# First attention of a hybrid kernel: the roots of the router's norms moved from GpSimd to VectorE, and GpSimd's row transfers unpaced

## The chip, the cores and the metric

One core of a Trainium2 chip runs the whole program. The time is the device time of one execution in microseconds (us), as the median of several runs. A profile comes from one execution of its own. Engines are called by their names or by the profile's: PE (TensorE), DVE (VectorE), ACT (ScalarE), POOL (GpSimd), SP (SyncE, which only issues transfers here).

## The reference, cut to what matters

```python
x = L0_attn_a_x                                        # [16, 256, 128]
x = x + attn_a(layernorm(x), mask, w_q, w_k, w_v, w_o)  # 16 sequences, one head of 128
x = x + ffn(layernorm(x), ...)                          # mixture of 8 experts, top 2, and a shared one
x = x + attn_b(layernorm(x), ...)                       # 16 causal heads of 8
x = x + ffn(layernorm(x), ...)

def layernorm(x):                                       # eps = 1e-5
    return (x - mean(x)) / sqrt(var(x) + eps)

def ffn(x, ...):
    logits = x @ router_w                               # [4096, 8]
    # first and second expert of each row, its place in that expert's list (capacity 1280)
    combine, dispatch = top2_gating(logits, capacity)
    y = combine-weighted silu(x_e @ w1 + b1) @ w2 + b2  # per expert, over the rows sent to it
    return y + 0.1 * (silu(x @ sw1 + sb1) @ sw2 + sb2)
```

## The kernel before, in words

All 4096 rows of x stay in SBUF, as 32 tiles of 128 rows. The 16 sequences of the first attention are taken in 8 pairs; one pair is 4 tiles. The order of work on every engine is written out by hand: each engine has its own `attn_a_pair(i)` (PE from line 856, ACT from 1248, DVE from 1721), called for i = -2 to 7, and each runs its instructions strictly in that order, with semaphores between the engines.

In step i the engines work on several pairs at once. Sequence n = 2i and n + 1 get their probabilities transposed and multiplied with the values, n + 1 and n + 2 get their scores, n + 2 and n + 3 are projected. Behind the attention runs the router of the mixture, also pair by pair:

- In step i DVE takes the statistics of pair i after its attention was added (`stats2`, and `stats2_end`, line 1510, which writes `mv2`, mean and variance of 4 tiles).
- GpSimd makes the inverse roots `rstd2` from them (`rstd2_of`, line 587: an add of epsilon and a power of -0.5, on 128 x 4 numbers).
- In step i + 1 DVE normalizes the four tiles into `xr` (`norm_r`, line 1519, four instructions of which the first waits for the root), PE transposes them (`r_transpose`, line 816, the matmuls on line 825), ACT copies them, PE makes the logits (`r_logits`, line 832), DVE finds the first expert (`lead`, five small operations) and then the second (`second`, line 1557, eight small operations), each of which waits on a semaphore for the one before.
- In step i + 2 PE counts the places of the rows (`counts`) and DVE makes the slot numbers (`placed`, line 1588, five small operations). In that step they are interleaved with the four `norm_r` of the next pair: placed, norm, placed, norm and so on.
- GpSimd then sends the rows: `dispatch(0, k)`, line 596, k = 0 to 63. Each is one indirect transfer of 128 rows of `xr` to their slots in `x_slots` in HBM, eight per pair (four tiles, first and second expert). In `attn_a` (line 630) GpSimd starts with the roots of the first norms and of the first two router norms; then a loop over i = 2 to 7 places five to seven transfers per pair behind waits for the probabilities' transposes, projections and values of that pair, and the root of the next pair behind them. The transfers left over follow at the end.

The last pair's router work lies in the first items of the mixture (`moe`, DVE from line 1848).

The mixture of a layer runs over 56 items of 256 rows: 16 pieces through the shared expert and 40 chunks, five per expert, through the experts. The first ten items are pieces (0 to 9), then come the 40 chunks, then the last six pieces. PE does `first_mm(w)` (line 919, in 12 matmuls) and then `second_mm(w - 1)` (line 940, in 16). DVE splits the input of item w + 1 in a high and a low part (`x_split`, line 1704) and adds the output of item w - 1 (`y_copy`, line 1831). In step w = 9, ahead of the first chunk, DVE's order is the other way round: `y_copy` of item 8 (line 1856), and then `x_split` of chunk 0, which for a chunk also transposes it (line 1714).

The chunks are read back from `x_slots` by SP (`chunk_loads`) and, for half of the first chunk, ACT (`first_chunk`), once all 64 row transfers have landed.

In the second attention the router's roots stay with GpSimd (`rstd2_of`, `shift2_of`) in both kernels.

Of the kernel before, what the change touches and what calls it, by code (L numbers as in the profile page):

```python
# [51 lines left out]
LEAD, SECOND, PLACED = 5, 8, 5  # L52
LIMITS, GATES = 7, 14
# [37 lines left out]
def build(nc, x_in, hd_mask, w_q, w_k, w_v, w_o, attn_W, attn_b, out_W, out_b, router_w,  # L91
          w1, b1, w2, b2, sw1, sb1, sw2, sb2, out):
    with ExitStack() as ctx:
# [76 lines left out]

        x_cols = sb("x_cols", [P, 2, CH * P])
# [82 lines left out]
        S.xg_used = sem("xg_used")  # L254
        S.row_set = sem("row_set")
# [237 lines left out]
        def _(pool):  # L493
# [85 lines left out]
            def shift2_of(i):  # L579
# [4 lines left out]
                pool.wait_ge(S.ln2_rstd, PAIRS + i + 1)  # L584
                pool.tensor_tensor(nb2[:, :], nm2[:, :], rstd2[:, :], ALU.mult).then_inc(S.ln2_nb, 1)

            def rstd2_of(n):
                pool.wait_ge(S.ln2_mv, n)
                if n > PAIRS + 1:

                    pool.wait_ge(S.xn2_ready, n - 1)
                pool.tensor_scalar(ve2[:, :], mv2[:, :, 1], EPS, 1.0, ALU.add, ALU.mult).then_inc(S.ln2_ve, 1)
                pool.wait_ge(S.ln2_ve, n)
# [36 lines left out]
            def attn_a():  # L630
# [8 lines left out]
                for q in range(2, 7):  # L639
                    rstd_of(q, q + 1)  # L640
                rstd2_of(1)
                rstd_of(7, 8)
                rstd2_of(2)
                k = 0

                def row():
                    nonlocal k
                    dispatch(0, k)
                    k += 1


                for i in range(2, PAIRS):
                    n = 2 * i
                    if i > 2:
                        pool.wait_ge(S.probs_tr, n + 1)
                        row()
                        pool.wait_ge(S.gv_done, min(n + 3, SEQS))
                        row()
                    pool.wait_ge(S.y_done, n + 1)
                    row()  # L660
                    pool.wait_ge(S.probs_tr, n + 2)
                    row()
                    pool.wait_ge(S.gv_done, min(n + 4, SEQS))
                    row()
                    pool.wait_ge(S.y_done, n + 2)
                    row()
                    if i > 2:
                        row()
                    rstd2_of(i + 1)

                for k in range(k, 2 * NT):
                    dispatch(0, k)
# [807 lines left out]
        def _(dve):  # L1480
# [37 lines left out]

            def norm_r(n, j):
                t = 4 * (n % PAIRS) + j  # L1520
                if j == 0:
# [5 lines left out]
                    dve.wait_ge(S.ln2_rstd, n + 1)  # L1527
# [193 lines left out]
            def attn_a_pair(i):  # L1721
                n = 2 * i
                routed, led = valid(i - 2), valid(i - 1)
                if valid(i):
                    inverse_sums(n)
                if 0 <= n + 1 < SEQS:
                    maxes(n + 1)
                if valid(i):
                    add_attn(n)
                for j in range(PLACED):  # L1730
                    if routed:
                        placed(i - 2, j, bank[2])
                    if led and j < 4:
                        norm_r(i - 1, j)
# [399 lines left out]
```

## Time and profile before

| | |
|---|---|
| median of 3 runs | 770.65 us (766.17 to 772.09) |
| the profiled execution | 770.89 us |
| its span in the profile | 769.1 us |
| PE busy | 704.7 us (92%), 6152 matmuls |
| DVE busy | 523.9 us (68%), 1665 instructions |
| ACT busy | 449.7 us (58%) |
| POOL busy | 440.9 us (57%), 564 instructions |

The span runs from the first to the last instruction of the profiled execution; the device time adds 1.8 us around it. Busy time is the time in which an engine executes, its waits are left out. Shares are means over stages with different limits, so the rows below are taken from the stages that the change touches: the first attention (till about 103 us), the pieces (till about 138 us) and the start of the chunks (143 us).

### The profile page before, as it was taken

To read this page: it belongs to the slowest core of one execution; us is meant where nothing else is said; L and a number is where in the kernel's file an instruction comes from. 1 tells how busy PE (TensorE), PEld (TensorE's weight loads), DVE (VectorE), ACT (ScalarE), POOL (GpSimd) and SP (SyncE) were. 2 spreads that over 40 slices of the span, in tenths; PEclk is the share of its full clock that TensorE was granted. 3 is DMA by queue.
4 is the path that set the end of the run, shared out by engine and by line. 5 is a ranking of instruction groups with operands and counts; after the bars stand their busy time and mean duration, and the time that the engine had idled before them with its cause. 6 is when DMAs were issued, how large, how long until landed. Compare 5 with 4: busy or idle time off the path is not lost.

```text
span 769.1 us, 18168 instructions
## 1 busy us (share of the span) xinstructions
PE 704.7 (92%) x6152; PEld 641.6 (83%) x6152; DVE 523.9 (68%) x1665; ACT 449.7 (58%) x1144; POOL 440.9 (57%) x564
## 2 busy tenths in 40 slices
PE   6888789799999997889999998999999899999996
PEld 5777689799999996667777776777779899999996
DVE  5877765366556565768888988877676556655536
ACT  2565454344444443677878878787755444456545
POOL 6367777166666651344545767777777265666640
PEclk9999869999999998899999999999999999999999
DMA  7997111455556334333533434333201346555328
GB/s 245 309 323 183 46 48 55 58 113 108 108 99 133 78 104 118 104 99 109 142 101 91 126 119 147 100 95 111 62 30 53 53 84 131 109 97 112 90 68 287
DMA packets 167715, 89.35 MB, mean 116 GB/s; under 512 B 120576, under 2 KB 151890, under 8 KB 167528
## 3 DMA queue, kind: packets, MB, share of 16 engines
q1 hardware_dynamic: 155704, 69.89, 36.6%
q0 software_dynamic: 9216, 17.34, 6.6%
q10 hardware_dynamic: 2704, 0.98, 0.6%
q8 instruction: 50, 0.82, 0.5%
q14 instruction: 41, 0.34, 0.1%
HBM read 49.63 MB, written 39.67 MB: 116 GB/s over the span
## 4 chain that ended last, share of the span: by engine, by line
PE 57%; DVE 5%; POOL 5%; DMA 5%; SPq 4%; issue 4%; ACT 3%; ACTq 0%; DVEq 0%; POOLq 0%
PE bank L940 22%; PE bank L919 19%; PE bank L1021 4%; DMA qc<-qk_rows 3%; SPq L439 3%; POOL x_slots L611 3%; PE bank L980 2%; PE bank L998 2%; PE bank L1002 2%; POOL pt L695 2%; DVE negp L1951 1%; PE bank L976 1%; PE bank L981 1%; ACT pt L1389 1%; PE bank L1040 1%
## 5 line engine op out<-in xcount | busy, mean ns | idle before, releaser
L1291 ACT ACTIVATE hT<-bank,bias_T 128x256 f32<-128x256 f32 x448 | 175.7, 476 | 186.4 <-PE bank L919 186.3
L626 POOL DMA_INDIRECT y_rows<-yo,row_cur x160 | 158.5, 990 | 127.9 <-DVE yo L1845 103.2
L1951 DVE TENSOR_REDUCE negp<-bank 128x2 f32<-128x512 f32 (+1 forms) x192 | 129.6, 685 | 44.3 <-PE bank L981 27.1
L940 PE MATMUL bank<-w_s,hT 128*128 128x128 f32 x1280 | 155.9, 275 | 0.0
L611 POOL DMA_INDIRECT x_slots<-xr,slot_u x128 | 129.9, 1015 | 38.7 <-issue 35.5
L940 PEld LDWEIGHTS bank<-w_s,hT 128*128 128x128 f32 x1280 | 150.0, 192 | 0.0
L919 PE MATMUL bank<-xT_hl,w_hl 128*128 128x256 f32 x960 | 135.4, 291 | 9.1 <-DVE xT_hl L1719 9.1
L695 POOL TENSOR_SCALAR_AFFINE_SELECT pt<-pt 128x512 f32<-128x512 f32 x128 | 86.0, 680 | 92.7 <-ACT pt L1389 92.2
L1389 ACT ACTIVATE pt<-bank 128x512 f32<-128x512 f32 x192 | 107.8, 596 | 40.3 <-PE bank L1002 38.5
L919 PEld LDWEIGHTS bank<-xT_hl,w_hl 128*128 128x128 f32 x960 | 120.9, 192 | 9.6 <-issue 9.6
L1845 DVE TENSOR_TENSOR yo<-bank,b_b 128x256 f32<-128x256 f32 x80 | 33.9, 424 | 98.7 <-PE bank L940 98.7
L940 PE MATMUL bank<-sw_s,hT 128*128 128x128 f32 x512 | 63.0, 276 | 2.1 <-issue 2.1
L940 PEld LDWEIGHTS bank<-sw_s,hT 128*128 128x128 f32 x512 | 60.2, 193 | 2.8 <-issue 2.8
L1021 PE MATMUL bank<-pt,v_ext 128*32 128x256 f32 (+1 forms) x1024 | 55.5, 335 | 6.6 <-POOL pt L695 6.4
L919 PE MATMUL bank<-xT_hl,sw_hl 128*128 128x256 f32 x384 | 55.5, 296 | 2.1 <-issue 1.5
L919 PEld LDWEIGHTS bank<-xT_hl,sw_hl 128*128 128x128 f32 x384 | 49.8, 198 | 2.9 <-issue 2.1
L1021 PEld LDWEIGHTS bank<-pt,v_ext 128*32 128x32 f32 x1024 | 26.9, 110 | 27.8 <-POOL pt L695 10.4
L980 PE MATMUL bank<-bdk,qc 96*128 96x256 f32 x128 | 48.9, 382 | 1.1 <-DVE negp L1951 0.4
L998 PE MATMUL bank<-qc,bdk 128*128 128x256 f32 x256 | 41.5, 284 | 0.2 <-ACT pt L1389 0.2
L980 PEld LDWEIGHTS bank<-bdk,qc 96*128 96x128 f32 x128 | 25.6, 200 | 17.2 <-issue 8.7
L976 PE MATMUL bank<-bdk,qc 128*128 128x512 f32 x64 | 31.6, 493 | 8.9 <-DMA qc<-qk_rows 8.6
L1002 PE MATMUL bank<-qc,bdk 128*128 128x128 f32 x256 | 37.0, 267 | 2.9 <-ACT pt L1389 2.9
(214 smaller groups left out, 1194.0 us busy)
## 6 DMA issues: line engine op xcount, KB each, us to landing
xg_all<-x_slots SPq DMA_DIRECT2D x316, 32.0 KB
w_s<-in_L_ffn_w SPq DMA_DIRECT2D x32, 256.0 KB
qk_rows<-qks SPq DMA_DIRECT2D x16, 512.0 KB, 3.6
bdk<-qk_rows SPq DMA_DIRECT2D x187, 32.0 KB
qc<-qk_rows SPq DMA_DIRECT2D x45, 128.0 KB, 2.8
x_slots<-xg_all SPq DMA_DIRECT2D x1, 5440.0 KB, 21.7
y_rows<-xg_all SPq DMA_DIRECT2D x1, 4096.0 KB, 14.3
yab<-y_rows SPq DMA_DIRECT2D x16, 256.0 KB, 3.3
```

Source lines behind the costliest of these rows:

```text
L611: pool.indirect_dma_start(x_slots, bass.IndirectOffsetOnAxis(ap=slot_u[:, c, t:t + 1], axis=0), xr[:, t, :], None, bounds_check=last_slot, ...
L626: pool.indirect_dma_start(y_rows, bass.IndirectOffsetOnAxis(ap=row_cur[:, g % ROWS, j:j + 1], axis=0), yo[:, g % RING, j, :], None, bounds ...
L695: a = pool.affine_select(out=blk, in_=blk, compare_op=ALU.is_ge, fill=0.0, base=0, pattern=[[0, 4], [1, P]], channel_multiplier=-1)
L919: m = pe.matmul(bk[:, (f % 2) * 256:(f % 2) * 256 + 256], wt[:, wp, f * P:(f + 1) * P], xT_hl[:, w % 2, xp, :], start=(p == 0), stop=(p == 2))
L940: m = pe.matmul(yb(w, l)[:, j * P:(j + 1) * P], hT[:, w % 2, f, j * P:(j + 1) * P], wt[:, f, :], start=(f == 0), stop=(f == FT - 1))
L980: pe.matmul(halves[:, :, 0:P], q[0:96], heads[0:96, :, 0:P], start=True, stop=True)
L998: m = pe.matmul(bk[:, j * SEQ:j * SEQ + SEQ], bdk[:, par, g, 2 * k + j, 0:P], qc[:, par, g, :], start=True, stop=True)
L1002: m = pe.matmul(bk[:, j * P:j * P + P], bdk[:, par, g, j, P:SEQ], qc[:, par, g, P:SEQ], start=True, stop=True)
L1021: m = pe.matmul(OB[32 * j:32 * j + 32, c0 + kt * P:c0 + SEQ], v_ext[:, par, kt, 4 * g + j, :], rhs, start=(kt == 0 and g % 2 == 0), stop=( ...
L1291: a = act.activation(hT[:, w % 2, f, :], HB[2 * (w % 2) + f // 2][:, (f % 2) * 256:(f % 2) * 256 + 256], ACT.Silu, bias=bias_T[:, b0 + f:b ...
L1389: act.activation(pt[:, g % 2, k, :], CB[(g + k) % 2][:, :], ACT.Exp).then_inc(S.exp_done, 1)
L1951: dve.tensor_reduce(dst, AB[(g + k) % 2][:, :].rearrange("p (j k) -> p j k", j=heads), AX.X, ALU.max, negate=True).then_inc(S.amax_done, 1)
```

## The change

GpSimd's `attn_a` keeps the eight roots of the first norms and then issues the 64 transfers one after another, with no wait but those inside `dispatch` (for the pair's slot numbers). The eight roots of the router's norms of the first layer are made by DVE: `root_of(n, k)`, k = 0 to 8. Step 0 adds epsilon; step 1 makes a seed from the bits of the number, read as an integer (times -0.5 plus a constant, written as an integer); steps 2 to 5 are one refinement of higher order and steps 6 to 8 a second one. Each works on 128 x 4 numbers and each but the first waits for the one before through the semaphore `root`. They are interleaved with the other work of the pair: 0 and 1 at the end of step i, 2 to 8 in step i + 1. The four norms, which stood between the placing steps, come behind them. Beside this, the counts that GpSimd waits for in the second layer are shifted by eight.

```diff
--- before.py
+++ after.py
@@ -50,6 +50,8 @@
 WB_LOADS = 11
 QUAD = 4 * P
 LEAD, SECOND, PLACED = 5, 8, 5
+ROOT = 9
+ROOT_BITS = float(0x5F3759DF)
 LIMITS, GATES = 7, 14
 START = 4
 BY_SP = 7
@@ -168,6 +170,7 @@
         oT = sb("oT", [P, GRP, SEQ])
         on = sb("on", [P, 2, HEADS, HD]); onT = sb("onT", [P, SEQ]); osum = sb("osum", [P, 2, HEADS])
 
+        root_y = sb("root_y", [P, 2, 4]); root_t = sb("root_t", [P, 2, 4])
         x_cols = sb("x_cols", [P, 2, CH * P])
         xT_hl = sb("xT_hl", [P, 2, 2, CH * P], F32R)
         sw1_hl = sb("sw1_hl", [P, 2, F], F32R)
@@ -252,6 +255,7 @@
         S.slots2_even = sem("slots2_even")
         S.slots2_odd = sem("slots2_odd")
         S.xg_used = sem("xg_used")
+        S.root = sem("root")
         S.row_set = sem("row_set")
         S.xT_hi = sem("xT_hi")
         S.xT_ready = sem("xT_ready")
@@ -581,16 +585,14 @@
                 need(pool, S.xn2_ready, PAIRS + i)
                 pool.tensor_scalar(nm2[:, :], mv2[:, :, 0], -1.0, 1.0, ALU.mult, ALU.mult).then_inc(S.ln2_nm, 1)
                 pool.wait_ge(S.ln2_nm, i + 1)
-                pool.wait_ge(S.ln2_rstd, PAIRS + i + 1)
+                pool.wait_ge(S.ln2_rstd, i + 1)
                 pool.tensor_tensor(nb2[:, :], nm2[:, :], rstd2[:, :], ALU.mult).then_inc(S.ln2_nb, 1)
 
             def rstd2_of(n):
                 pool.wait_ge(S.ln2_mv, n)
-                if n > PAIRS + 1:
-
-                    pool.wait_ge(S.xn2_ready, n - 1)
+                pool.wait_ge(S.xn2_ready, n - 1)
                 pool.tensor_scalar(ve2[:, :], mv2[:, :, 1], EPS, 1.0, ALU.add, ALU.mult).then_inc(S.ln2_ve, 1)
-                pool.wait_ge(S.ln2_ve, n)
+                pool.wait_ge(S.ln2_ve, n - PAIRS)
                 pool.tensor_tensor(rstd2[:, :], ve2[:, :], neg_half[:, :], ALU.pow).then_inc(S.ln2_rstd, 1)
 
             def dispatch(l, k):
@@ -636,39 +638,9 @@
                 pool.wait_ge(S.ln_rstd, 2)
                 key_ones()
                 query_masks()
-                for q in range(2, 7):
+                for q in range(2, 8):
                     rstd_of(q, q + 1)
-                rstd2_of(1)
-                rstd_of(7, 8)
-                rstd2_of(2)
-                k = 0
-
-                def row():
-                    nonlocal k
-                    dispatch(0, k)
-                    k += 1
-
-
-                for i in range(2, PAIRS):
-                    n = 2 * i
-                    if i > 2:
-                        pool.wait_ge(S.probs_tr, n + 1)
-                        row()
-                        pool.wait_ge(S.gv_done, min(n + 3, SEQS))
-                        row()
-                    pool.wait_ge(S.y_done, n + 1)
-                    row()
-                    pool.wait_ge(S.probs_tr, n + 2)
-                    row()
-                    pool.wait_ge(S.gv_done, min(n + 4, SEQS))
-                    row()
-                    pool.wait_ge(S.y_done, n + 2)
-                    row()
-                    if i > 2:
-                        row()
-                    rstd2_of(i + 1)
-
-                for k in range(k, 2 * NT):
+                for k in range(2 * NT):
                     dispatch(0, k)
 
             def attn_b_consts():
@@ -1516,6 +1488,32 @@
                     a = dve.bn_aggr(mv2[:, j, :], st2[:, j, :])
                 a.then_inc(S.ln2_mv, 1)
 
+            def root_of(n, k):
+
+                y, t = root_y[:, 0, :], root_t[:, 0, :]
+                if k == 0:
+                    dve.wait_ge(S.ln2_mv, n + 1)
+                    a = dve.tensor_scalar(ve2[:, :], mv2[:, :, 1], EPS, None, ALU.add)
+                else:
+                    dve.wait_ge(S.root, ROOT * n + k)
+                if k == 1:
+                    a = dve.tensor_scalar(y.bitcast(I32), ve2[:, :].bitcast(I32), -0.5, ROOT_BITS, ALU.mult, ALU.add)
+                elif k == 2:
+                    a = dve.tensor_tensor(t, ve2[:, :], y, ALU.mult)
+                elif k == 3:
+                    a = dve.tensor_tensor(root_t[:, 1, :], t, y, ALU.mult)
+                elif k == 4:
+                    a = dve.scalar_tensor_tensor(out=t, in0=root_t[:, 1, :], scalar=-10.0 / 3.0, in1=root_t[:, 1, :], op0=ALU.add, op1=ALU.mult)
+                elif k == 5:
+                    a = dve.scalar_tensor_tensor(out=root_y[:, 1, :], in0=t, scalar=5.0, in1=y, op0=ALU.add, op1=ALU.mult)
+                elif k == 6:
+                    a = dve.tensor_tensor(t, ve2[:, :], root_y[:, 1, :], ALU.mult)
+                elif k == 7:
+                    a = dve.scalar_tensor_tensor(out=root_t[:, 1, :], in0=t, scalar=-0.5 * 0.375 ** 3, in1=root_y[:, 1, :], op0=ALU.mult, op1=ALU.mult)
+                elif k == 8:
+                    a = dve.scalar_tensor_tensor(out=rstd2[:, :], in0=root_t[:, 1, :], scalar=0.5625, in1=root_y[:, 1, :], op0=ALU.add, op1=ALU.mult)
+                a.then_inc(S.root, 1)
+
             def norm_r(n, j):
                 t = 4 * (n % PAIRS) + j
                 if j == 0:
@@ -1524,7 +1522,10 @@
                         dve.wait_ge(S.slots1, 512)
                         dve.wait_ge(S.slots2_even, 256)
                         dve.wait_ge(S.slots2_odd, 256)
-                    dve.wait_ge(S.ln2_rstd, n + 1)
+                    if n < PAIRS:
+                        dve.wait_ge(S.root, ROOT * (n + 1))
+                    else:
+                        dve.wait_ge(S.ln2_rstd, n - PAIRS + 1)
                 a = dve.tensor_scalar(xr[:, t, 0:D], x[:, t, :], mv2[:, j, 0:1], rstd2[:, j:j + 1], ALU.subtract, ALU.mult)
                 if j == 3:
                     a.then_inc(S.xn2_ready, 1)
@@ -1723,14 +1724,23 @@
                 routed, led = valid(i - 2), valid(i - 1)
                 if valid(i):
                     inverse_sums(n)
+                if led:
+                    root_of(i - 1, 2)
                 if 0 <= n + 1 < SEQS:
                     maxes(n + 1)
+                if led:
+                    root_of(i - 1, 3)
                 if valid(i):
                     add_attn(n)
+                if led:
+                    root_of(i - 1, 4)
                 for j in range(PLACED):
                     if routed:
                         placed(i - 2, j, bank[2])
                     if led and j < 4:
+                        root_of(i - 1, 5 + j)
+                if led:
+                    for j in range(4):
                         norm_r(i - 1, j)
                 if i == 0:
                     stats(4, 5)
@@ -1787,7 +1797,12 @@
                     stats2_end(i)
                 if led:
                     second(i - 1, 6)
+                if valid(i):
+                    root_of(i, 0)
+                if led:
                     second(i - 1, 7)
+                if valid(i):
+                    root_of(i, 1)
 
             for i in range(-2, PAIRS):
                 if i == -1:
@@ -1850,6 +1865,8 @@
                 for w in range(start, upto):
                     c = w - FRONT[l]
                     if l == 0 and w == 0:
+                        for k in range(2, ROOT):
+                            root_of(last, k)
                         for j in range(4):
                             norm_r(last, j)
                     if c == -1:
```

## Rows read from the trace of the kernel before

**Rows 1.** Busy time by engine (us, with instructions), PEclk granted clock; a middle and the last pair, chunk start
```profile
59.58:69.73 10.15, 8.70 (x69) 8.04 (x69) 8.15 (x44) 6.04 (x18) 8.02 (x9) 1.00 0.91 218
...
90.95:103.00 12.05, 8.78 (x42) 7.69 (x43) 8.00 (x42) 3.82 (x9) 8.28 (x9) 0.52 0.14 46
...
143.00:148.00 5.00, 5.00 (x32) 5.00 (x33) 1.42 (x5) 1.57 (x4) 0.00 (x0) 0.70 0.44 56
```

**Rows 2.** The chain that ended last: start us, us, what; 135 to 151
```profile
135.47 2.57 DMA x_slots<-xr,slot_u
...
141.50 0.46 DVE x_cols L1714
...
142.99 2.90 PE bank L919 x12
145.90 1.89 PE bank L940 x16
147.78 1.43 PE bank L919 x12
149.21 1.79 PE bank L940 x16
```

**Rows 3.** Timeline of PE around the first chunk: start us, us, line, operation, idle before
```profile
135.84 1.95 PE L940 MATMUL bank<-sw_s,hT 128*128 128x128 f32 x16
142.99 2.26 PE L919 MATMUL bank<-xT_hl,w_hl 128*128 128x256 f32 x9 [5.21 <-DVE xT_hl L1719]
```

**Rows 4.** GpSimd's transfers and roots, VectorE's norms by tile (ns min/median/max); one transfer
```profile
L611 POOL DMA_INDIRECT x_slots<-xr,slot_u x64: 967/974/1212, 42.9 to 135.5; - x64
...
L1528 DVE TENSOR_SCALAR xr<-x,mv,rstd x32: 331/340/528, 30.9 to 104.8; 128x128 f32<-128x128 f32 x32
...
L594 POOL TENSOR_TENSOR rstd<-ve,neg_half x8: 1009/1039/1040, 29.0 to 103.0; 128x4 f32<-128x4 f32 x8
...
64.90 0.97 POOL L611 DMA_INDIRECT x_slots<-xr,slot_u  x1 [0.30 <-issue]
```

**Rows 5.** Timeline of VectorE, the last pair's routing and before the first chunk
```profile
104.08 1.30 DVE L1528 TENSOR_SCALAR xr<-x,mv,rstd 128x128 f32<-128x128 f32 x4 [1.10 <-POOL rstd L594]
...
106.68 0.28 DVE L1599 TENSOR_REDUCE RR<-sel 128x16 f32<-128x128 f32 x1
107.00 0.17 DVE L1602 TENSOR_SCALAR far<-RR 128x8 f32<-128x8 f32 x1
107.21 0.16 DVE L1604 SCALAR_TENSOR_TENSOR slot_u<-RR,far 128x4 uint32<-128x4 f32 x1
...
117.38 0.18 DVE L1607 TENSOR_TENSOR slot_u<-RR,far 128x4 uint32<-128x4 f32 x1
...
137.83 0.42 DVE L1838 SCALAR_TENSOR_TENSOR x<-bank,x 128x256 f32<-128x256 f32 x1 [2.19 <-PE bank L940]
```

**Rows 6.** Timeline of VectorE, a middle pair of the first attention
```profile
59.50 0.16 DVE L1687 RECIPROCAL rsum<-psums 128x2 f32<-128x2 f32 x1
59.58 0.67 DVE L1682 TENSOR_REDUCE negmax<-bank 128x2 f32<-128x512 f32 x1
...
60.69 0.27 DVE L1595 TENSOR_TENSOR sel<-MK,bank 128x128 f32<-128x128 bf16 x1
...
62.12 0.34 DVE L1528 TENSOR_SCALAR xr<-x,mv,rstd 128x128 f32<-128x128 f32 x1
...
62.92 0.69 DVE L1682 TENSOR_REDUCE negmax<-bank 128x2 f32<-128x512 f32 x1 [0.30 <-PE bank L793]
```

**Rows 7.** Timeline of PE, the router's transposes of pair 1 and of a middle pair
```profile
32.22 0.60 PE L825 MATMUL bank<-ident,xr 128*128 128x128 f32 x4
...
62.72 0.60 PE L825 MATMUL bank<-ident,xr 128*128 128x128 f32 x4
```

**Rows 8.** Timeline of VectorE, pair 1
```profile
30.40 0.61 DVE L1694 SCALAR_TENSOR_TENSOR x<-bank,rsum,x 128x128 f32<-128x128 f32 x2 [1.08 <-PE bank L812]
30.93 1.11 DVE L1528 TENSOR_SCALAR xr<-x,mv,rstd 128x128 f32<-128x128 f32 x4
```

## The prediction

> **What bounds the kernel now.** I first read the busy time of each engine in three stretches [rows 1]: in a middle pair of the first attention (59.58 to 69.73) PE is busy 8.70 of 10.15 us at a granted clock of 1.00, VectorE 8.15. In the last pair the clock is 0.52. In the 5 us behind the start of the expert chunks it is 0.70. Then the chain that ended last [rows 2]: it runs along GpSimd's row transfers to the last one, issued at 135.47, on through its landing and the load of chunk 0 to VectorE's transpose at 141.50, and comes to PE at 142.99. From there on PE holds the chain, two products per item. PE's timeline shows what that costs [rows 3]: it stood idle for 5.21 us before the first chunk. So two things in this part set the end: the time when the attention and the ten pieces ahead of the chunks are through on PE, and the hole in front of chunk 0. From 142.99 on nothing that the diff touches in the first router is late.
>
> GpSimd's own rows [rows 4] say how full it is: 64 transfers from 42.9 to 135.5, each 0.97 us with 0.30 of issue ahead, so 1.27 apart; eight roots of 1.04 us stand among them (each with a small add before it).
>
> **Edit 1: GpSimd loses the eight roots and the paced waits.** Its 64 rows alone want 64 x 1.27 = 81.3 us. What stops them then is VectorE's placing of a pair. The last four indices of the last pair come at 117.38 [rows 5], and eight rows behind that take 10.2 us: last row issued at some 127 instead of 135.47, if VectorE's times stay. From the last issue to chunk 0 on PE it took 7.5 us (135.47 to 142.99, from [rows 2]), so rows alone would let chunk 0 start near 134.5.
>
> But they don't start it alone. In front of chunk 0 VectorE first runs y_copy of item 8 (line 1856), which waits for PE's second product of item 8, the very last PE work ahead of the hole [rows 3, 5]: VectorE waited 2.19 us for it and ran it at 137.83 for 0.42 us. Behind it come transpose, high part and low part: 141.50 to 142.99 is 1.49 us. So the earliest start of chunk 0 relative to the pieces is 137.83 + 0.42 + 1.49 = 139.74, and the hole shrinks by 142.99 - 139.74 = 3.25 us, not by 5.21. The other 1.96 us stay. Second gain: the first twelve products behind the hole took 2.90 us and the sixteen after them 1.89, against 1.43 and 1.79 an item later [rows 2]: 1.57 us of half clock. I count all of it as saved, since in the middle pairs, with waits of one to two us in every ten, the clock stood at 1.00 [rows 1]; the bound below is nothing saved. Gain together: 3.25 + 1.57 = 4.8 us (3.3 to 4.8). Margin: the rows have (139.74 - 134.5), some 5 us, before they decide again; a later attention shifts both sides alike.
>
> **Edit 2: nine small operations per pair on VectorE, in order, and the four normalizations moved behind the placing.** Prices: a small operation between others that it doesn't depend on costs 0.08 us (rsum at 59.50, next at 59.58 [rows 6]); one that waits for the one before costs 0.21 (107.00 to 107.21 [rows 5]).
> - Steps 0 to 2, at the end of a pair and before the maxima: some 0.2 us in front of the maxima (bounds 0.16 for two hidden ones, 0.6 for three serial ones).
> - Steps 3 and 4 add 2 x 0.08 = 0.16 before the placing.
> - Steps 5 to 8 take the place of the norms between the five placing steps. Those alone are spaced 0.32 (106.68 to 107.00) and 0.21 [rows 5], and I take 0.31 for the first; with one small step in each gap the last root step starts near 0.92 and is through at 1.13. Then four norms of 0.26 apart and the 0.34 of the last: 2.25 us from the first placing step to the last norm's end. Before, they ran between 60.69 and 62.46, 1.77 us [rows 6]. So 0.48 more.
> - Norm end against the maxima: 0.16 + 0.48 = 0.64 later. PE's transposes for the router (line 825) started at 62.72, 0.26 after the last norm's end [rows 7], of which 0.06 is the semaphore: 0.20 of reserve. PE stalls 0.44 us, in order, so all that is behind it stalls too: projection, logits, values, and VectorE's lead step, which waits for the logits. Per middle pair 0.44 + 0.20 = 0.64 us; there are five (i = 2 to 6): 3.2 us.
> - Pair 1: no placing to hide in. VectorE waited 1.08 us for the values [rows 8], which hides steps 2 and 3; steps 4 to 8 are serial, 5 x 0.21 = 1.05, before norms that ran from 30.93. PE's transposes there started at 32.22 [rows 7], with 0.18 since the norms' end: 0.9 us.
> - Pair 7: PE at half clock, no reserve assumed: 0.64 + 0.20 = 0.8 us.
> - Last pair's norms (in the mixture's item 0): before, VectorE waited 1.10 us for GpSimd's root [rows 5]. Now seven serial steps, 7 x 0.21 = 1.47, stand there: 0.4 us more.
> Sum: 0.9 + 3.2 + 0.8 + 0.4 = 5.3 us later when the pieces begin, and as PE is busy through the ten pieces, when they end. Bounds: from below 2 us, if the small steps fall into VectorE's waits (it sits idle in each pair before its second maxima [rows 6] and its lead step); from above every step serial, five more in the open at 0.13 each in seven pairs, 4.5 us on top: 9.8.
> GpSimd's wait that went costs nothing elsewhere: of the eight roots only the last has VectorE's norms waiting for it in the timeline [rows 5].
>
> Two rules of the Trainium skill speak against this. The row first: the 32 norms took 331 at least, 340 in the middle and 528 ns at most, with GpSimd busy beside them all the time [rows 4], so a collision cost up to 0.19 us and was rare. The Trainium skill (GPSIMD Engine Reference, Key points) says that GpSimd shares its SBUF interfaces with VectorE and collides with instructions that have two SBUF inputs; six of the nine steps have two. By that rule the edit costs more; it is a rival below. The Trainium skill (VectorE: DVE Perf Modes, The DRAIN you can't avoid) says that the next operation doesn't start until the pipe is empty; the row at 59.50 shows 0.16 us of duration and the next start after 0.08, so the trace agrees only for dependent steps.
>
> **Sum.** The profiled execution took 770.89 us (span 769.1); it lies 0.2 from the median of the three runs, 770.65. 770.9 - 4.8 + 5.3 = 771.4 us: what GpSimd gives back VectorE takes. Both terms lie ahead of a part that PE bounds, so none is absorbed later.
>
> **Rivals.**
> - A, cheap steps: the lead step sets the cadence, small steps fall into waits, 2 us lost: 770.9 - 4.8 + 2 = 768. For it: VectorE has 2 us of idle time per pair [rows 1]. Against: the chain goes through the norms' end to PE with only 0.20 of reserve. If also PE keeps its full clock in pair 7, some 2 more: 766.
> - B, serial steps: 5.3 + 4.5 = 9.8 us lost: 775.9. For it: every step waits on a semaphore of the one before. Against: others stand between most of them.
> - C, the clock, on the other side: PE's added waits in each pair bring it down to 1.2 GHz in the middle pairs too. The pair at 0.52 took 12.05 us against 10.15, though it had 42 products and not 69 [rows 1]: at least 1.9 us more in each of five pairs, 9.5: 781. It decides as soon as one middle pair shows a clock under 1. Against: pairs with PE idle 1.4 us in 10 stood at 1.00, and 2.1 is near that.
> - D, contention: each two-input step (6 x 8 = 48) pays 0.19: 9.1 us: 780.5. Against: the median of 340 above.
> - E, the change doesn't do what it says: the rows' end still starts chunk 0, nothing of the hole saved: 770.9 + 5.3 = 776. Against: 5 us of margin.
>
> **Chances.** Forecast (769 to 774) 0.52; A 0.23; B 0.09; C 0.08; D 0.03; E 0.05. What a measurement of this kernel can tell from no change is about 1%, 7.7 us. Slower by more takes C or D, or half of these together with B: 0.11. Faster by more would take A without any loss and a better clock: 0.03. Same: 0.86. Range: 766 (A with the clock) to 778 (B and E, and a part of C), with 0.09 left above and 0.05 below.
>
> **What would show it.** Right: PE's hole before the first chunk near 2 us, behind VectorE's x split that waits for the second product of item 8 and not for a load; twelve products at 1.43 us at once; last row issued well over 5 us before the pieces end; pairs of 10.8 us; PE's line 825 waiting for the norms in each; chunk 0 starting between 142 and 145. Wrong: pairs of 10.2 (A), a clock under 1 in pairs 2 to 5 (C), small steps of over 0.3 us (D), root steps 0.21 apart throughout (B), a hole over 4 us (E).

## The result, and the profile after

The kernel after took 774.29 us in the median of 17 runs (770.69 to 780.38), the one before 769.88 in the median of 17 beside it: a ratio of 1.0048, 95% interval 1.0026 to 1.0069. By the ratio the kernel after is 3.7 us slower (2.0 to 5.3); the medians lie 4.4 apart. The ratio is of the fast runs alone, and one of the 17 of the kernel before, at 2349.93 us, was a slow one. The time lies in the range given, on the slow side of the 771.4 forecast. The profiled execution of after took 772.18 us (span 770.4), 1.3 more than that of before.

VectorE's timeline in the first attention, kernel after (start us, us, line, operation; line 1683 is the maxima, 1502 and 1504 are root steps 2 and 3, 1596 the first placing step, 1514 root step 8, 1529 the four norms as one group):

```profile
61.75 0.16 DVE L1502 TENSOR_TENSOR root_t<-ve,root_y 128x4 f32<-128x4 f32 x1
61.83 0.68 DVE L1683 TENSOR_REDUCE negmax<-bank 128x2 f32<-128x512 f32 x1
62.43 0.18 DVE L1504 TENSOR_TENSOR root_t<-root_t,root_y 128x4 f32<-128x4 f32 x1
...
63.13 0.27 DVE L1596 TENSOR_TENSOR sel<-MK,bank 128x128 f32<-128x128 bf16 x1
...
64.04 0.15 DVE L1514 SCALAR_TENSOR_TENSOR rstd<-root_t,root_y 128x4 f32<-128x4 f32 x1
...
64.23 1.11 DVE L1529 TENSOR_SCALAR xr<-x,mv,rstd 128x128 f32<-128x128 f32 x4
...
72.72 0.68 DVE L1683 TENSOR_REDUCE negmax<-bank 128x2 f32<-128x512 f32 x1
...
75.09 1.33 DVE L1529 TENSOR_SCALAR xr<-x,mv,rstd 128x128 f32<-128x128 f32 x4
```

It answers to [rows 6]. The maxima come at 61.83 and again at 72.72: 10.89 us, where the pair of [rows 1] took 10.15. From the first placing step (63.13) to the end of the fourth norm (64.23 + 1.11 = 65.34) it is 2.21 us; the prediction had 2.25. But the norms at 75.09 took 1.33 us, not 1.11. That was not foreseen.

PE's timeline, kernel after (line 797 transposes for the router, 891 and 912 are the two products of an item):

```profile
32.70 0.66 PE L797 MATMUL bank<-ident,xr 128*128 128x128 f32 x4 [0.60 <-DVE xr L1529]
...
65.40 0.66 PE L797 MATMUL bank<-ident,xr 128*128 128x128 f32 x4 [0.26 <-DVE xr L1529]
...
76.48 0.66 PE L797 MATMUL bank<-ident,xr 128*128 128x128 f32 x4 [0.45 <-DVE xr L1529]
...
99.33 1.12 PE L797 MATMUL bank<-ident,xr 128*128 128x128 f32 x4 [0.85 <-DVE xr L1529]
...
106.29 2.90 PE L891 MATMUL bank<-xT_hl,sw_hl 128*128 128x256 f32 x12 [1.37 <-issue]
...
111.32 1.12 PE L797 MATMUL bank<-ident,xr 128*128 128x128 f32 x4 [1.60 <-DVE xr L1529]
...
141.73 1.95 PE L912 MATMUL bank<-sw_s,hT 128*128 128x128 f32 x16
146.74 1.66 PE L891 MATMUL bank<-xT_hl,w_hl 128*128 128x256 f32 x12 [3.06 <-DVE xT_hl L1720]
```

It answers to [rows 3, 7]. PE now waits for the norms in every pair: 0.24 to 0.47 us in the middle ones, 0.60 in pair 1, 0.85 in pair 7. The last product ahead of the first chunk begins at 141.73, against 135.84: 5.89 us later. The hole is 3.06 us, against 5.21. The chain that ended last, kernel after, from the hole on:

```profile
142.49 2.67 DMA xg_all<-x_slots
145.25 0.46 DVE x_cols L1715
...
146.74 1.66 PE bank L891 x12
148.41 1.79 PE bank L912 x16
150.19 1.43 PE bank L891 x12
```

The twelve products behind the hole take 1.66 us, not 2.90 [rows 2]: the granted clock was 1.00 from 143 to 150, where it was 0.70 before [rows 1]. The second item's products begin at 150.19, against 147.78: 2.41 us later, and the second attention's first product comes at 309.00, against 306.26, 2.74 later. GpSimd's timeline, kernel after:

```profile
42.69 1.21 POOL L613 DMA_INDIRECT x_slots<-xr,slot_u  x1 [7.48 <-DVE slot_u L1608]
...
113.80 0.97 POOL L613 DMA_INDIRECT x_slots<-xr,slot_u  x1 [5.49 <-DVE slot_u L1608]
...
133.55 0.97 POOL L613 DMA_INDIRECT x_slots<-xr,slot_u  x1 [0.30 <-issue]
```

The last row goes out at 133.55, 8.2 us ahead of the start of PE's last product before the hole (141.73). The rows have ceased to bind, and GpSimd stood idle for 5.49 us in front of pair 6.

### The profile page after: what moved, and what is told of

The parts are those of the page before. It is cut to its first block, busy times and chain, and to the rows that moved or that the text cites. A ratio compares the mean times of both kernels' runs of the same rounds, so it can differ in the third digit from the quotient of the medians.

```text
span 770.4 us, 18218 instructions
## 1 busy us (share of the span) xinstructions
PE 704.2 (91%) x6152; PEld 639.4 (83%) x6152; DVE 532.3 (69%) x1737; ACT 449.1 (58%) x1144; POOL 430.3 (56%) x548
## 4 chain that ended last, share of the span: by engine, by line
PE 65%; DVE 14%; issue 4%; DMA 4%; POOL 4%; SPq 3%; ACT 3%; ACTq 0%; DVEq 0%; POOLq 0%
PE bank L912 24%; PE bank L891 20%; PE bank L993 4%; DMA qc<-qk_rows 3%; SPq L443 3%; PE bank L952 2%; PE bank L970 2%; PE bank L974 2%; POOL pt L667 2%; DVE negp L1968 2%; POOL x_slots L613 1%; PE bank L804 1%; DVE xr L1529 1%; PE bank L948 1%; PE bank L953 1%
## 5 line engine op out<-in xcount | busy, mean ns | idle before, releaser
L1853 DVE SCALAR_TENSOR_TENSOR x<-bank,x 128x256 f32<-128x256 f32 x32 | 13.5, 422 | 38.3 <-PE bank L912 38.2
```

## The experiments

All ratios are to the kernel before, timed beside each. An effect of 1 or 2 us is about as wide as their intervals, so there the traces are read, by stage. Each kernel has one trace, so a reading of a time far behind the change (the start of the second attention) is weak: before_split_first and the kernel before, which should not differ, stand 2.6 us apart there (303.70 and 306.26).

**1. act_early.** ACT's two loads for chunk 0 stood behind its activations of piece 9.

```diff
-                    if w == FRONT[l]:
+                    if w == FRONT[l] - (l == 0):
                         first_chunk(l)
                     silus(l, w)
```

> The kernel after, with ACT's half of chunk 0's load issued ahead of the activations of piece 9 and not behind them. My theory: of PE's 3.06 us hole in front of the first chunk 1.1 us are ACT's, which issued its two loads at 142.09 only when piece 9 was through. Then the hole falls to 1.9 to 2.1 us, chunk 0 starts 1.1 us earlier against the pieces, and VectorE's transpose waits for no load. Rival: SP's half or the landing itself ends last; then the hole stays at 3.0. Time against the kernel after: 1 us less by the first, nothing by the second.

The ratio is 1.0005 (0.9965 to 1.0044); the interval overlaps that of the kernel after, so the 1 us expected is not resolved by time. In the kernel after, ACT's own queue (line 1278 is the load) looks like this:

```profile
142.09 0.35 ACTq L1278 DMA_DIRECT2D xg_all<-x_slots  x1
...
142.49 0.79 ACTq L1278 DMA_DIRECT2D xg_all<-x_slots  x1
```

and in act_early, with PE below it:

```profile
136.97 0.35 ACTq L1278 DMA_DIRECT2D xg_all<-x_slots  x1
...
137.36 0.46 ACTq L1278 DMA_DIRECT2D xg_all<-x_slots  x1
```

```profile
139.82 1.95 PE L912 MATMUL bank<-sw_s,hT 128*128 128x128 f32 x16
143.63 1.67 PE L891 MATMUL bank<-xT_hl,w_hl 128*128 128x256 f32 x12 [1.86 <-DVE xT_hl L1720]
```

Against PE's last product ahead of the hole the first load goes out 2.85 us before it (136.97 to 139.82) and not 0.36 us behind it (141.73 to 142.09). VectorE's transpose waits for no load, and PE's hole is 1.86 us instead of 3.06. So 1.2 us of the hole were ACT's queue, as expected; the 1.86 left are the 1.96 that the prediction had worked out.

**2. split_first.** The same, and at w = 9 of the first layer VectorE splits chunk 0 before it takes over item 8's output.

```diff
-                    if c == -1:
+                    if c == -1 and l == 1:
                         y_copy(l, w - 1)
...
-                    if w > 0 and c != -1:
+                    if w > 0 and not (c == -1 and l == 1):
                         y_copy(l, w - 1)
```

> As act_early, and VectorE prepares chunk 0 before it takes over item 8's output. My theory: the remaining 1.96 us of the hole are y_copy and the split of chunk 0 behind PE's last product; with the order turned the hole is under 0.3 us, and the first chunk starts some 3 us earlier against the pieces than in the kernel after. Time: 3 us under the kernel after, so within 1 us of the kernel before. Rival: the rows or their loads are still the later ones; then a hole of 1 to 2 us stays.

The ratio is 0.9999 (0.9968 to 1.0030). PE's timeline in it:

```profile
142.28 1.95 PE L912 MATMUL bank<-sw_s,hT 128*128 128x128 f32 x16
143.99 1.68 PE L891 MATMUL bank<-xT_hl,w_hl 128*128 128x256 f32 x12
```

No wait stands at the first chunk's row. The 3.06 us of the hole were 1.2 of ACT's order and 1.9 of VectorE's order; the rows had no part.

**3. before_split_first**, the control: both edits on the kernel before.

> The kernel before with chunk 0's load and split as in split_first, roots and rows as before: a control. There the rows end last, so neither order decides: PE's hole stays at 5 to 5.4 us and the time is that of the kernel before within 0.3%. Rival: the order was what held chunk 0 in the kernel before too; then the hole is 2 to 3.5 us.

The ratio is 1.0001 (0.9978 to 1.0024). VectorE's timeline (line 1714 is chunk 0's transpose):

```profile
138.97 0.45 DVE L1714 STREAM_TRANSPOSE x_cols<-xg_all 128x256 f32<-128x256 f32 x1 [6.69 <-DMA xg_all<-x_slots]
```

It waits 6.69 us for the load, and PE's hole is 6.03 us, over the band that I gave since the pieces ended earlier in this execution (last product at 132.49, last row at 133.66). The rows and their load hold chunk 0 in the kernel before, and neither order does.

**4. norms_late.** The kernel before with the four norms behind the placing steps; GpSimd keeps the roots.

```diff
                 for j in range(PLACED):
                     if routed:
                         placed(i - 2, j, bank[2])
-                    if led and j < 4:
+                if led:
+                    for j in range(4):
                         norm_r(i - 1, j)
```

> The kernel before, with only the place of the four norms changed: behind the five placing steps, in pairs 1 to 7; GpSimd keeps the roots. My theory: the norms end some 0.3 us later against the maxima, PE has 0.2 of reserve, so a middle pair costs 0.1 to 0.2 us more (10.3), and chunk 0 still starts when the rows are in, near 143.5. Rival: the place of the norms is most of the 0.7 us that a pair became longer; then pairs of 10.6 or more.

The ratio is 1.0018 (0.9979 to 1.0057). VectorE's maxima:

```profile
49.54 0.67 DVE L1682 TENSOR_REDUCE negmax<-bank 128x2 f32<-128x512 f32 x1
...
59.88 0.67 DVE L1682 TENSOR_REDUCE negmax<-bank 128x2 f32<-128x512 f32 x1
```

10.34 us, and from pair 2's maxima to pair 7's (39.13 to 91.81) 52.68 us, against 51.72 before: 0.19 per pair, as expected.

**5. steps_beside.** The kernel before with the nine steps added at their places, on tiles of their own; nobody reads the result.

> The kernel before with the nine root steps added on VectorE at the places that they have in the kernel after, from their own tiles and with a result that nobody reads; the norms stay between the placing steps and wait for GpSimd's root, GpSimd is untouched. My theory: steps 0 to 2 (0.2 us), 3 and 4 (0.16) and 5 to 8 (0.3) push norms and maxima: middle pairs of 10.5 to 10.7, so the steps and not the new place of the norms are most of the cost. Rival: the steps fall into waits, pairs of 10.2 to 10.3. Time: 3 to 5 us more than before by the first, as the hole in front of chunk 0 shrinks by what the attention grows until VectorE's order holds it; near before by the second.

The ratio is 1.0041 (1.0010 to 1.0073). VectorE's maxima:

```profile
50.21 0.68 DVE L1712 TENSOR_REDUCE negmax<-bank 128x2 f32<-128x512 f32 x1
...
60.79 0.68 DVE L1712 TENSOR_REDUCE negmax<-bank 128x2 f32<-128x512 f32 x1
```

10.58 us; over five pairs (39.66 to 93.00) 53.34 us, 0.32 more per pair than before. The same sum for the kernel after is 39.97 to 95.57, 55.60 us, 0.78 more per pair. Steps and place together make 0.51 of the 0.78, and steps are the larger part.

Some 0.27 us per pair belong to neither alone. Most of it is PE's reserve of 0.20 us, which each edit alone can use in full, while the two together have it only once. Against the maxima, PE's transposes start 3.14 us later before (59.58 to 62.72), 3.26 in norms_late (59.88 to 63.14), 3.25 here (60.79 to 64.04) and 3.57 in the kernel after (61.83 to 65.40, a pair whose norms took 1.11): 0.12 and 0.11 alone, 0.43 together. The longer norms of the other pairs come on top, see the next run.

The hole in front of chunk 0 did not shrink by what the attention grew, as I had expected: it is 4.74 us. The last row goes out at 138.64, 3.2 us later than before: with its roots and rows still in one queue behind the attention's work, GpSimd moved back by as much as the attention grew.

**6. rows_after_norms.** split_first, and GpSimd's first row of a pair waits for the norms that VectorE writes behind the placing.

```diff
                     if c == 0:
                         pool.wait_ge(S.placed, PLACED * (n + 1))
+                        if l == 0 and q < PAIRS - 2:
+                            pool.wait_ge(S.xn2_ready, q + 2)
```

> split_first, and GpSimd holds the first row of each of pairs 0 to 5 until the norms of the next pair are written. In the kernel after, the fourth norm takes 0.52 and not 0.34 us where GpSimd's first row of the pair ends in it; both start from the same placing step, so they meet in most pairs. My theory: then no norm meets a row's end, all four together take 1.11 us, and middle pairs are 10.8 us throughout, not 10.8 to 11.0 and 11.8; the rows still are in before the pieces end. Rival: the 0.2 us have nothing to do with the rows; pairs stay as in the kernel after.

The ratio is 0.9960 (0.9927 to 0.9993). The four norms in split_first, and then in rows_after_norms:

```profile
64.53 1.33 DVE L1529 TENSOR_SCALAR xr<-x,mv,rstd 128x128 f32<-128x128 f32 x4
...
75.60 1.34 DVE L1529 TENSOR_SCALAR xr<-x,mv,rstd 128x128 f32<-128x128 f32 x4
```

```profile
63.76 1.12 DVE L1531 TENSOR_SCALAR xr<-x,mv,rstd 128x128 f32<-128x128 f32 x4
...
74.58 1.12 DVE L1531 TENSOR_SCALAR xr<-x,mv,rstd 128x128 f32<-128x128 f32 x4
```

In split_first the norms of all five pairs from 53 us to 99 us take 1.33 or 1.34 us; with the row held all five take 1.11 or 1.12. Two middle pairs go from 11.07 to 10.81 and 10.84 us (61.39 to 72.20 to 83.04), the last one from 11.81 to 11.37. Five pairs take 55.05 us (39.36 to 94.41) against 55.82 in split_first (40.26 to 96.08), 0.15 per pair.

But the expectation was right in part only. The first two of the five pairs take 11.04 and 10.99 us, not 10.8. And the norms still meet a row's end; it is another norm and another row. The row before the held one, the last of the pair in front, now ends in the third norm (64.28 to 64.77 in the pair at 63.76):

```profile
63.75 0.97 POOL L615 DMA_INDIRECT x_slots<-xr,slot_u  x1 [0.30 <-issue]
L1531 DVE TENSOR_SCALAR xr<-x,mv,rstd x20: 339/343/504, 52.9 to 97.6; 128x128 f32<-128x128 f32 x20
```

(The second line is of the view by tile: least, median and greatest duration in ns.) The third norm, in the last of the five pairs the first, takes 0.47 to 0.50 us, but the next starts 0.26 behind it as ever, so the block of four is no longer for it. In the first two pairs a row's end also meets root step 0 (0.37 us at 49.71, not 0.16) or a placing step (0.34 at 52.29, not 0.17). The edit moves the meetings, it does not end them; it pays because the fourth norm, for which PE waits, is out of the way.

**7. held_only.** That edit alone, on the kernel after.

> The kernel after, with only the first row of each of pairs 0 to 5 held until the norms of the next pair are written. It tells how much of what the kernel after lost is the meeting of norms and rows. My theory: middle pairs of 10.8 us, the last one of 11.4 in place of 11.8, 1.0 to 1.5 us in all, so chunk 0 starts near 145.5 in place of 146.7, and the time lies 1 to 1.5 us under the kernel after: a ratio of 1.002 to 1.004 to the kernel before. Rival: the gain seen with rows_after_norms is chance; ratio 1.005 as the kernel after.

The ratio is 1.0016 (0.9988 to 1.0045), under the 1.0048 of the kernel after, but the intervals overlap, so neither the expectation nor its rival is out by time. In the trace the five pairs take 55.03 us (40.22 to 95.25) against 55.60: 0.57 us, not the 1.0 to 1.5 expected. PE's timeline:

```profile
143.26 1.66 PE L893 MATMUL bank<-xT_hl,w_hl 128*128 128x256 f32 x12 [2.51 <-DVE xT_hl L1722]
```

Chunk 0 starts 3.5 us earlier than in the kernel after, more than the pairs explain (maxima of pair 7 at 95.25 against 95.57). Of the rest 0.55 us are a shorter hole (2.51 for 3.06), as ACT's load landed in 2.07 us and not in 2.67. The other 2.6 us come with the clock. Busy time and clock (the column behind the engines) of the kernel before, of the kernel after, and then of held_only, each for its whole stretch at half clock around the last pair:

```profile
91.37:108.43 17.06, 12.46 (x60) 11.15 (x58) 10.81 (x52) 5.99 (x14) 12.20 (x14) 0.50 0.11 38
```

```profile
97.17:114.23 17.06, 12.36 (x57) 11.06 (x58) 11.78 (x61) 5.11 (x12) 8.35 (x9) 0.50 0.10 34
```

```profile
101.12:107.94 6.82, 5.35 (x28) 4.86 (x27) 6.16 (x34) 2.30 (x5) 5.30 (x6) 0.50 0.16 55
```

PE stood at 1.2 GHz for 6.8 us here and for 17.1 us in the kernel after, and just as long in the kernel before. Over all thirteen traces this stretch is 6.8 to 17.1 us long (in hybrid6 there are two of 6.8), with either kind of root in the short and in the long ones: it moves a single trace by some us and says nothing of the edit.

**8. pool_unpaced.** The kernel before without the paced waits; between the roots stand as many rows as before, four in step 2 and seven in each later step.

> The kernel before without the paced waits alone; the roots stay on GpSimd, the same numbers of rows between them. My theory: GpSimd was full except for two waits of 0.7 and 1.2 us, so the last row goes out 1 to 2 us earlier and chunk 0 starts that much earlier: the pacing was worth 1 to 2 us at most, the roots the rest. Rival: rows that start earlier push a root later, norms wait, and the attention grows by as much.

The ratio is 1.0003 (0.9971 to 1.0034). From the first pair's maxima to the last row it is 107.3 us (27.87 to 135.19), against 106.8 before (28.63 to 135.47). I had expected 1 to 2 us; the pacing was worth nothing here, so what GpSimd gave back in the kernel after were the roots.

**9. front11_full.** The kernel before with 11 pieces ahead of the chunks, and the two orders of split_first.

```diff
-FRONT = (10, 10)
+FRONT = (11, 10)
```

> The kernel before, with one more piece ahead of the chunks (11 in place of 10) and chunk 0's load and split as in split_first; roots and norms as before. The piece fills 3.2 of the 5.2 us of the hole, a hole of some 2 us stays, at full clock. The first chunk starts where it started, 1.6 us of half clock are saved; at the end of the layer one piece less stands behind the chunks, and the second attention starts on what depends on the last rows' return, so of the 3.2 us at most 1 comes through: 1.6 to 2.7 us under the kernel before. Rival: all of the 3.2 us come through: 4.8 us under it.

The ratio is 0.9984 (0.9952 to 1.0016), in which both no gain and the 1.6 to 2.7 us of the first expectation lie. PE's hole is 1.40 us, and at 142.10 the chunks begin. The second attention begins at 304.07, 2.2 us earlier than in the kernel before, but not earlier than in before_split_first (303.70), which has no extra piece: the trace shows no gain of its own. The 4.8 us of the rival lie outside the interval.

**10. hybrid6.** split_first, but GpSimd makes the roots of pairs 0 to 5 and VectorE those of 6 and 7.

> GpSimd makes the roots of pairs 0 to 5 again (between its rows, without paced waits), VectorE only those of pairs 6 and 7; norms between the placing steps for pairs 0 to 5; chunk 0's load and split as in split_first. My theory: rows need only be in when the pieces are through. GpSimd's work from its first row at 42.9 is 64 x 1.27 + 4 x 1.5 = 87.3 us, so the last row goes out near 130; the attention grows by 1 to 1.5 us (the pair with the root of pair 6, and the last norms) and not by 5.9. Pieces end near 139.3, no hole (under 0.5 us), twelve products at 1.43 at once: 5 us under the kernel before, some 765. Rival: the shorter hole was not worth that, or other waits of the second attention take it back: within 2 us of the kernel before.

The ratio is 0.9977 (0.9945 to 1.0008). PE's timeline:

```profile
137.05 1.95 PE L923 MATMUL bank<-sw_s,hT 128*128 128x128 f32 x16
138.76 1.68 PE L902 MATMUL bank<-xT_hl,w_hl 128*128 128x256 f32 x12
```

The first chunk starts at 138.76 with no hole, 8 us earlier in its trace than in that of the kernel after, and the last row goes out at 130.14, as expected. The 5 us under the kernel before were not reached: by the ratio it is 1.8 us, within the rival's 2, and the second attention starts at 305.11, only 1.2 us earlier than in the kernel before. A part of what took it back stands in VectorE's timeline, at the split of expert 2's weights:

```profile
169.79 0.43 DVE L1847 CAST w_hl<-w_s 128x512 fp32r<-128x512 f32 x1 [3.02 <-DMA w_s<-in_L_ffn_w]
```

SP issued those weights at 163.87 and 164.35, behind 11 chunks' loads of some 2.45 us each (two of them took 3.3 us or more); the second landed 5.42 us later. PE waited 1.81 us behind it, and from 174.13 to 177.54 its granted clock was 0.50. At its first product of the second attention PE then waited 3.1 us for data, against 1.63 before.

**11. hybrid6_w.** hybrid6 with those two loads one chunk earlier in SP's order.

```diff
-                    if c % CHUNKS == 1 and CHUNKS < c < NCH - CHUNKS:
+                    if l == 0 and c == CHUNKS:
+                        weights(2)
+                    elif c % CHUNKS == 1 and CHUNKS < c < NCH - CHUNKS and not (l == 0 and c == CHUNKS + 1):
                         weights(E * l + c // CHUNKS + 1)
```

> hybrid6, with the two loads of expert 2's weights issued one chunk's loads earlier by SP (after the loads of chunk 10, not 11). In hybrid6 VectorE waited 3.02 us for these weights and PE 1.81, which gave back what the earlier start of the chunks had won. SP needs 2.45 us for one chunk's loads, so they go out that much earlier. My theory: VectorE's wait falls under 1 us, PE has no wait there, the second attention starts 2 to 4 us earlier than in hybrid6 (301 to 303 in place of 305.1), 3 us under hybrid6's time. Rival: the landing was slow (5.42 us) because other transfers were ahead of it, and is as slow then; VectorE waits 1 to 3 us still, and no time is won.

The ratio is 0.9954 (0.9933 to 0.9975), 767.09 us in the median: 3.5 us under the kernel before by the ratio, and the lowest of all, though rows_after_norms (0.9960) cannot be told from it. VectorE waits for these weights no more. They were issued 1.5 us earlier (162.36 and 162.81) and landed by 166.48, within 3.7 us and not 5.42; why they landed faster no run shows. VectorE waits 2.20 us for the next expert's weights instead, PE 0.65 us behind that, and PE's first product of the second attention comes at 302.13, as expected:

```profile
302.13 0.77 PE L961 MATMUL bank<-bdk,qc 128*128 128x512 f32 x1 [1.98 <-DMA qc<-qk_rows]
```

## Why the prediction was right, and where it was off

The forecast was that gain and loss cancel, 771.4 us, within 1%. The measured 774.3 is within it and within the range of 766 to 778, but 0.3 above the 769 to 774 that the forecast itself stood for, and the slowdown of 2.0 to 5.3 us does not hold the 0.5 that was forecast. What gains and what loses was right; three terms were set too favourably. Term by term:

- **Rows no longer bind.** Right: last row at 133.55, and split_first shows that nothing of the hole was theirs. The prediction had 127 for VectorE's old times; with the attention's 5.3 that is 132.
- **Middle pairs, 5 x 0.64 = 3.2 us.** Measured 55.60 - 51.72 = 3.88. In a pair whose norms took 1.11 us the working held: the block from placing to the last norm 2.21 for 2.25, PE's transposes 0.43 later against the maxima for 0.44, small steps between others near 0.08 apart (61.75 to 61.83); such pairs grew by 0.68 and 0.74 us. It was short by what it had set aside as rival D: a collision with GpSimd, which it priced at the root steps and gave 0.03. (It counted six steps with two inputs; the diff has seven, steps 2 to 8.) No root step was lengthened by more than 0.05 us in the kernel after: step 2 took 161 to 164 ns in all eight pairs. The fourth norm was, by 0.22 us in three of these five pairs and in the last, and PE's transposes then came 0.61 to 0.65 us later against the maxima, not 0.41 to 0.43.
- **Pair 1, 0.9.** The five serial steps cost what was said: norms 1.50 us behind the addition (30.03 to 31.53), against 0.53 [rows 8], so 0.97. But the values had come 0.37 earlier, which hid a part: the transposes came 0.48 later (32.70 for 32.22) and the next pair's maxima 0.74 (39.97 for 39.23).
- **Pair 7, 0.8; the last norms, 0.4.** Measured 1.06 (from the maxima, 95.57 to 106.29, against 90.95 to 100.61 in the trace of before) and 0.21 (106.29 to 111.32, against 100.61 to 105.43).
- **Sum 5.3.** Measured 5.89 at the last product of item 8.
- **The hole, 1.96 left.** This is the step that failed most ("The other 1.96 us stay"): it was 3.06. The prediction listed what VectorE does in front of chunk 0, and took the load as there, since the rows were. It forgot that half of that load is in ACT's queue behind the activations of piece 9. VectorE waited 1.11 us for that load. act_early moved it and the hole fell to 1.86.
- **The clock, 1.57.** Measured 1.34 (4.79 us for the first 28 products before, 3.45 after). This is one trace's number: in the five traces with a hole of 4.7 to 6.2 us the products behind it ran at half clock for 2.9 to 6.2 us, in the eight with a hole of 3.1 us or less for none.
- **Net at the second item, +0.5.** Measured 5.89 - 2.15 - 1.34 = 2.40, and the traces stand 2.41 apart. The difference to the forecast is 1.1 of ACT's, 0.6 of the attention and 0.2 of the clock.

The 2.4 us lie inside the interval of the measured slowdown (2.0 to 5.3), so the terms may be all there is. By the middle of it, 3.7, 1.3 us are missing, and no run settles whether they exist: the half clock around the last pair is as long in one trace as in the other (17.1 us), the one behind the hole is longer in three of the other traces of the kernel before's kind than in its own, and the traces end only 1.3 us apart.

Rival A (cheap steps) is out: no middle pair under 10.8. Rival B (all serial) is out: the steps are 0.07 to 0.12 apart where others stand between. Rival C is out for the middle pairs: the clock was 1.00 in all of them, with 2 us of PE idle in each. Busy time by engine and clock, kernel after:

```profile
61.83:72.72 10.89, 8.93 (x70) 7.96 (x69) 8.88 (x53) 6.03 (x18) 7.61 (x9) 1.00 0.86 197
```

Rival D is out as it was priced, since no root step of the kernel after was held, though GpSimd did hold the norms. E is out by split_first.

## What to carry to other kernels

When a queue is the last to end, list every condition of the next consumer, on each engine that has a part in its load and preparation, before you count the gain: here the rows' 5 us of margin met two orders written out by hand that had never mattered. Moving work off a full engine pays only for as much as the consumer can take: with the two orders mended, two of the eight roots on VectorE were enough to close the hole, while all eight cost 5.9 us of attention. Yet all eight with the orders mended and one row per pair held (rows_after_norms, 0.9960) were as fast as two of eight without the move of the weights (hybrid6, 0.9977): where the small steps fall counts as much as how many there are. And where a stage starts earlier, look at the next queue: VectorE waited 0.4 us for expert 2's weights in the kernel before, 3.0 us when the chunks began earlier, and one place in SP's order took that away.

## What the runs showed that was not expected

Some VectorE instructions that run near the end of an indirect transfer's issue by GpSimd are held. In the kernel after the fourth norm of the pair at 75.09 ends at 76.42, 0.22 late, and so does the reciprocal behind it (0.30 us, not 0.15); the row that GpSimd began at 75.40 ends at 76.37:

```profile
75.40 0.97 POOL L613 DMA_INDIRECT x_slots<-xr,slot_u  x1 [0.95 <-DVE slot_u L1608]
```

Held were instructions of a few kinds, all with one tensor input from SBUF: norms, root steps 0 and 1 (0.37 and 0.39 us in held_only), the third placing step, reciprocals and casts. The reductions of the placing and the statistics, which have one too, were not (at 74.29 and 60.38 in the kernel after). Nor were the eight maxima across a row's end there, which read PSUM, nor instructions with two inputs: three root steps ran across a row's end there (at 52.84, 63.39 and 85.31) and took 0.15 to 0.16 us. A two-input root step was longer only right behind a held instruction (0.26 us at 52.37 in rows_after_norms). The fourth norm would have ended some 0.17 us before the row's end each time; in the pair at 64.23 it stood at the same distance and was not held, and why stays open.

The meetings were no fewer in the kernel before. There a row's end fell in the third placing step (0.30 to 0.41 us, not 0.16, in three of the five pairs) or in the third norm (0.52 us in the other two). None of these cost PE a wait, since other instructions stood between them and the block's end:

```profile
L1602 DVE TENSOR_SCALAR far<-RR x6: 160/230/407, 41.2 to 93.0; 128x8 f32<-128x8 f32 x6
```

In the kernel after, the pair's first row starts 0.31 us behind the start of the norms each time from the pair at 53.16 on: the last placing step releases the row, and the norms stand right behind that step on VectorE. So its end meets the last norm, which holding the row avoided (rows_after_norms), the one for which PE waits. The Trainium skill (GPSIMD Engine Reference, Key points) names contention of GpSimd with VectorE instructions in a 2-port perf mode or with two SBUF inputs. The norms have one tensor input, so of the two cases only the first could cover them, and no trace names an instruction's mode; for the second the traces show nothing, 145 to 182 ns for the root steps with two inputs in the kernel after.

The paced waits in GpSimd's order turned out to be worth nothing, though they look like care for VectorE: in pool_unpaced norms and pairs stayed as they were (maxima 10.16 to 10.21 us apart in the first three middle pairs, 10.15 to 10.20 before).
